# Eight PSUM banks in two sets that change roles: T5 attention with its scores in two groups and the projections behind the weighing

## The reference, cut to what matters

```python
q = (hidden_states @ wq).reshape(b, s, H, DK).transpose(0, 2, 1, 3)   # k and v likewise; H=16, DK=64, s=512
scores = jnp.einsum('bhqd,bhkd->bhqk', q, k) + bias                   # bias by relative position and head
attn = softmax(scores)
out = jnp.einsum('bhqk,bhkd->bhqd', attn, v)
return out.transpose(0, 2, 1, 3).reshape(b, s, H * DK) @ wo
```

## Time and profile before

| | |
|---|---|
| median of 3 runs | 1156.37 us (1152.84 to 1157.34) |
| the profiled execution | 1156.04 us, of which the span of its instructions 1154.2 us |
| mean granted TensorE clock | 0.997 |
| PE, DVE, ACT, POOL busy over the span | 97%, 79%, 80%, 54% |
| attention, from W0(0) to W0(29) | 60.48 to 402.15 us |

### The profile page before, as it was taken

The page is one execution under the profiler, slowest core; times in us unless marked ns, Lnnn a source line. Parts: engine busy times, 40 slices in busy tenths (PEclk is TensorE's granted clock), DMA queues, the critical chain, the costliest instruction groups (busy, mean ns, idle before and its releaser), DMA issues.

```text
span 1154.2 us, 40441 instructions
## 1 busy us (share of the span) xinstructions
PE 1121.6 (97%) x16041; PEld 721.5 (63%) x16041; DVE 911.5 (79%) x2424; ACT 924.6 (80%) x2455; POOL 617.7 (54%) x406
## 2 busy tenths in 40 slices
PE   8899999999999998999999999999999899999998
PEld 3367777677776763666666666555556566666665
DVE  4798989999999978887777777867778777777774
ACT  5887877777787868887888888887888788888975
POOL 4466666566666644764564555433353455655540
PEclk9999999999999999999999999999999999999999
DMA  8411111111111122311111111011010111110110
GB/s 276 172 39 40 58 41 54 44 49 49 40 58 40 57 74 63 93 38 31 31 44 42 29 43 34 20 34 33 19 42 20 35 28 43 43 42 20 43 43 20
DMA packets 30364, 58.36 MB, mean 51 GB/s; under 512 B 5680, under 2 KB 7152, under 8 KB 30176
## 3 DMA queue, kind: packets, MB, share of 16 engines
q1 hardware_dynamic: 30176, 55.77, 17.9%
HBM read 15.32 MB, written 1.11 MB: 14 GB/s over the span
## 4 chain that ended last, share of the span: by engine, by line
PE 83%; ACT 8%; issue 4%; DVE 3%; POOL 1%; DMA 1%; SPq 0%; DVEq 0%; ACTq 0%; POOLq 0%
PE ps L326 11%; PE ps L301 11%; PE ps L1501 6%; PE ps L1425 5%; PE ps L1458 5%; PE ps L1362 5%; PE ps L1372 4%; PE ps L1395 4%; PE ps L1363 4%; PE ps L1437 4%; PE ps L1465 4%; PE ps L337 3%; PE ps L1507 3%; ACT arena L1725 3%; PE ps L267 2%
## 5 line engine op out<-in xcount | busy, mean ns | idle before, releaser
L241 POOL TENSOR_TENSOR arena<-arena 128x1024 f32<-128x1024 f32 x128 | 241.0, 1893 | 144.9 <-DVE arena L536 144.8
L1302 POOL TENSOR_TENSOR arena<-arena 128x1024 f32<-128x1024 f32 x64 | 121.4, 1897 | 225.8 <-DVE arena L1903 225.8
L432 ACT ACTIVATE arena<-arena 128x512 f32<-128x512 f32 x256 | 182.4, 713 | 73.8 <-DVE arena L522 73.4
L1725 ACT ACTIVATE arena<-arena 128x128 f32<-128x128 f32 x512 | 198.2, 390 | 16.3 <-DVE arena L1895 15.7
L1895 DVE CUSTOM_DVE_ANT_0 arena<-ps,near,arena 128x128 f32<-128x128 f32 x512 | 144.5, 348 | 50.1 <-PE ps L1425 50.1
L522 DVE CUSTOM_DVE_ANT_0 arena<-ps,arena 128x512 f32<-128x512 f32 x256 | 164.3, 688 | 23.9 <-PE ps L301 21.1
L532 DVE STREAM_TRANSPOSE arena<-arena 128x1024 f32<-128x1024 f32 x128 | 157.8, 1234 | 1.1 <-POOL arena L241 0.9
L1309 POOL TENSOR_TENSOR arena<-arena 128x1024 f32<-128x1024 f32 x64 | 151.0, 2359 | 0.1
L326 PEld LDWEIGHTS ps<-arena 32*64 32x64 f32 x8192 | 118.8, 130 | 37.2 <-issue 36.7
L301 PE MATMUL ps<-arena 64*128 64x256 f32 (+1 forms) x736 | 138.4, 488 | 2.0 <-DVE arena L522 1.4
L326 PE MATMUL ps<-arena 32*64 32x128 f32 x8192 | 134.8, 274 | 0.5 <-issue 0.4
(11 more groups left out here) (164 smaller groups left out, 2179.0 us busy)
## 6 DMA issues: line engine op xcount, KB each, us to landing
arena<-arena SPq DMA_DIRECT2D x127, 128.0 KB, 2.3
arena<-arena SPq DMA_DIRECT2D x64, 192.0 KB, 2.6
arena<-rel_rows SPq DMA_DIRECT2D x16, 448.0 KB, 9.3
arena<-arena SPq DMA_DIRECT2D x64, 64.0 KB, 2.1
arena<-y SPq DMA_DIRECT2D x30, 128.0 KB, 2.3
arena<-arena SPq DMA_DIRECT2D x15, 127.8 KB, 2.4
arena<-in_wqkv SPq DMA_DIRECT2D x2, 768.0 KB, 5.1
x<-in_x SPq DMA_DIRECT2D x4, 256.0 KB, 4.7
```

Of the source, the lines that this page charges most:

```text
L241: nc.gpsimd.tensor_tensor(e, e, scale, ALU.mult).then_inc(self.normed, 1)
L432: nc.scalar.activation(self.e[:, r % 3, i, :], self.neg[:, i, :], ACT.Exp, bias=self.nmax[:, i:i + 1], scale=-1.0, accum_out=self.sums[:, ...
L1302: nc.gpsimd.tensor_tensor(e, e, self.rsum.unsqueeze(2).to_broadcast([P, H8, P]), ALU.mult).then_inc(self.p_normed, 1)
L1725: nc.scalar.activation(self.e[:, s, h, :], self.neg[:, h, :], ACT.Exp, bias=self.nmax[:, h:h + 1], scale=-1.0, accum_out=self.sums[:, s, h ...
```

## The change

The eight banks become two sets of four, `T5_S` and `T5_W`, whose roles depend on the unit. In slot u one set X takes the weighed output of unit u-1, the other set Y the scores of round r. When the biases of round r have read Y, its banks take Q, K, V(u+2) and PO(u-1). When out-copy(u-1) has read X, all four scores of round r+1 go to X. Unit 31 is excepted and stays in `T5_W`.

On PE both pairs of round r+1 stand together at the end of the slot, and Q, K, V come directly behind W1, ahead of PO. On ACT, exp(r+1,0) and exp(r+1,1) move behind the copies of q, k, v, and the two half copies of v move behind exp(r+1,3), as a function of their own. On DVE, from slot 1 on, four biases stand together in each round, the turns are shifted later by half a round, and add(u-1) stands ahead of bias(r+1,0) to bias(r+1,3). The closing slot's own order on DVE goes. The number of instructions for the arithmetic is the same.

```diff
+    def weigh_home(self, u):
+        return T5_S if u % 2 and u < self.LAST else T5_W
+    def score_home(self, r):
+        slot = r // 2 - 1
+        if slot <= 0:
+            return T5_S
+        return self.weigh_home(slot - 1) if r % 2 else self.other_home(slot)
+    def other_home(self, slot):
+        return T5_W if self.weigh_home(slot - 1) == T5_S else T5_S
...
         def q_proj(u):
-            if u >= 1:
+            if 1 <= u <= 2:
                 pe.wait_ge(self.q_read, u)
+            if u >= 3:
+                pe.wait_ge(self.biased, 8 * (u - 1) + 1)
+            Q = self.proj_banks(u)[0]
...
         def score(r, pair):
+            home, slot = self.score_home(r), u - 1
+            if pair == 0 and r % 2 and slot >= 1:
+                pe.wait_ge(self.ot_made, slot)
...
-                    if r >= 1 and c.start == 0:
+                    if r >= 1 and c.start == 0 and not (r % 2 and slot >= 1):
                         pe.wait_ge(self.biased, 4 * (r - 1) + i + 1)
...
         def weigh(u, half):
-                elif u >= 1:
-                    pe.wait_ge(self.added, u)
+                elif u == self.LAST - 1:
+                    pe.wait_ge(self.biased, 4 * (2 * self.LAST) + 3)
...
+                    if c == 0 and a == self.GROUPS - 1 and 1 <= u < self.LAST:
+                        pe.wait_ge(self.added, u)
...
-        def project_out(u, bank=T5_W):
+        def project_out(u):
             pe.wait_ge(self.ot_made, u + 1)
+            if u < self.LAST - 1:
+                pe.wait_ge(self.biased, 8 * (u + 2) + 4)
...
             if u >= 1:
                 weigh(u - 1, 1)
-            if scores:
+            if u == -1:
                 score(r + 1, 0)
-            if u >= 1:
-                project_out(u - 1)
             if u + 2 < self.UNITS:
                 q_proj(u + 2)
                 k_proj(u + 2)
                 v_proj(u + 2)
+            if u >= 1:
+                project_out(u - 1)
+            if u >= 0:
+                score(r + 1, 0)
             if scores:
                 score(r + 1, 1)
...
+        for u in range(1, self.UNITS - 1):
+            r = 2 * (u + 1)
+            if u >= 2:
+                invert_sums(r - 1, 0)
+                turn(r - 2, 1)
+                invert_sums(r - 1, 1)
+            for i in range(4):
+                add_bias(r, i)
+            invert_sums(r, 0)
+            if u >= 2:
+                turn(r - 1, 0)
+            turn(r - 1, 1)
+            invert_sums(r, 1)
+            turn(r, 0)
+            add_out(u - 1)
+            for i in range(4):
+                add_bias(r + 1, i)
+
+        r = 2 * (self.UNITS - 1)
+        invert_sums(r + 1, 0)
+        turn(r, 1)
+        invert_sums(r + 1, 1)
+        turn(r + 1, 0)
```

More of the change, by code:

```diff
@@ L218, in __init__, with proj_banks, out_bank @@
         self.weighed, self.ot_made, self.o_made, self.added = sem("weighed"), sem("ot_made"), sem("o_made"), sem("added")
+        self.LAST = self.UNITS - 1
         self.done, self.last = self.added, self.UNITS
+    def weigh_home(self, u):
[7 more added lines that the diff above has]
+        return T5_W if self.weigh_home(slot - 1) == T5_S else T5_S
+    def proj_banks(self, u):
+        slot = u - 2
+        first = T5_W + 1 if slot <= 0 else self.other_home(slot)
+        return tuple(self.k.ps[:, first + j, :] for j in range(3))
+    def out_bank(self, u):
+        if u >= self.LAST - 1:
+            return T5_W if u == self.LAST else T5_S + 3
+        return self.other_home(u + 1) + 3
     def sp(self, sp):
@@ L246, in pe @@
         k, nc, ps = self.k, self.k.nc, self.k.ps
-        Q, K, V = (ps[:, T5_W + j, :] for j in range(1, 4))
         ahead = self.ahead
@@ L325, in weigh @@
                         cols = slice(h * DK, (h + 1) * DK)
-                        last = nc.tensor.matmul(ps[cols, T5_W + a, 0:P], self.v[rows, u % 3, (a - c) % self.GROUPS, c // self.GROUPS, cols],
+                        last = nc.tensor.matmul(ps[cols, home + a, 0:P], self.v[rows, u % 3, (a - c) % self.GROUPS, c // self.GROUPS, cols],
                                                 self.pt[rows, u % 2 * 2 + h, :, keys],
@@ L412, in copy_k @@
                 act.wait_ge(self.scored, 8 * (u - 1))
-            nc.scalar.activation(self.kk[:, u % 2, :], K, ACT.Copy).then_inc(self.k_read, 1)
+            nc.scalar.activation(self.kk[:, u % 2, :], self.proj_banks(u)[1], ACT.Copy).then_inc(self.k_read, 1)
         def copy_v(u):
@@ L461, in act @@
                 exp(r, 3)
+            if scores and u < 0:
                 exp(r + 1, 0)
@@ L469, in act @@
                 copy_v(u + 2)
+            if scores and u >= 0:
+                exp(r + 1, 0)
+                exp(r + 1, 1)
             if scores:
@@ new lines, in add_out @@
+            nc.vector.tensor_tensor(xb, ps[:, self.out_bank(u), :], xb, ALU.add).then_inc(self.added, 1)
+        for u in range(-1, 1):
+            r = 2 * (u + 1)
+            for i in range(4):
+                add_bias(r, i)
+                if u == -1 and i == 0:
+                    ahead.norm4.scale(dve, 1)
+            if u == -1:
+                ahead.norm4.scale(dve, 2)
+            invert_sums(r, 0)
+            if u == -1:
+                ahead.norm4.scale(dve, 3)
+            else:
+                turn(r - 1, 1)
+            invert_sums(r, 1)
+            add_bias(r + 1, 0)
+            add_bias(r + 1, 1)
+            turn(r, 0)
+            invert_sums(r + 1, 0)
+            turn(r, 1)
+            add_bias(r + 1, 2)
+            add_bias(r + 1, 3)
+            turn(r + 1, 0)
+            invert_sums(r + 1, 1)
```

77 lines of the change are left out of this document (25 added, 52 removed).

## The result

The changed kernel takes 1149.86 us (median of 6 runs, 1148.11 to 1151.9), the kernel before beside it 1156.86 us (6 runs, 1152.84 to 1159.67). The ratio is 0.9935, with an interval of 0.9921 to 0.9950: faster by 0.65%, 7.0 us. The forecast was 1149.0.

The account below looks back on a forecast made before the run. PE was taken to set the pace, with DVE next. From 1156.04 us, -6.1 (steady slots), -2.0 (start) and +0.95 (end) sum to -7.15, giving 1148.9, written as 1149.0 us after a 0.33 us median offset; range 1146.5 to 1153.

Parts of the forecast that it names:

- What bounds the kernel: Steady slots: PE is gapless and sets the pace, a tiling switch costs about 0.2 us, DVE comes next.
- Part 1: Steady slots 1 to 29: five tiling switches instead of six save 0.21 us each, -6.1 us.
- W0 2.03: Steady slots: the first weighing block keeps its old length of 2.03 us in the new order.
- New waits in the steady slots: Steady slots: PE's new waits on DVE and ACT cost nothing; DVE waits at two places, about 0.9 us.
- the cover of 1.1 us: Steady slots: smallest margin before PE would wait for DVE, 1.1 us, at the add and at bias(r+1,3).
- Part 2: Start of attention: Q, K, V(2) fill PE's 1.44 us wait for a bias; -2.0 us, bounds -0.3 and -2.2.
- 1.5 for the order: Start: with only the bound from bias(3,3), W1(0) starts at 62.9 instead of 64.42, 1.5 us earlier.
- 0.5 for the half copies: Start: half copies of v behind exp(1,3) let DVE come forward, raising the gain from 1.5 to -2.0 us.
- The bound of 61.9: Start: S(4,1) must wait for bias(3,3), starting at 61.20 before with its result 0.69 later.
- The clock's fall at the start: Start: rival, chance 0.15; the clock falls again there, 1.7 us come back, giving 1150.7 us.
- Part 3: End, slot 30: W1(30) starts 13.5 behind W0(29), 12.57 before; loses +0.95 us, bounds 0 and +1.5.
- the two reasons given: End: PO(29) waits 0.85 us for the out-copy, and centre(0) waits for bias(63,3), out at 12.5.

Follow-up runs that it names:

- e1: Changed kernel with the scores of round r+1 split around PO, putting two tiling switches back; 1160.44 us, ratio 1.0024 to the kernel before.
- e7: Changed kernel with one extra DVE addition of 128 x 512, result unused, behind the add in slots 1 to 30; 1150.35 us, ratio 0.9929.
- e8: Changed kernel with three extra DVE additions of 128 x 512, results unused, behind the add in slots 1 to 30; 1181.09 us, ratio 1.0205.
- e10: Changed kernel with 32 matmuls of 8 columns, results unused, added at the head of the kernel; 1161.22 us, ratio 1.0034.
- e12: Changed kernel with 32 unused matmuls of 8 columns at its head and turn(62,0) moved behind the last four biases; 1160.70 us, ratio 1.0033.
- e4: Changed kernel with PE's wait for add(u-1) at the head of W0 instead of its seventh matmul; 1151.16 us, ratio 0.9941.
- e9: Changed kernel with the attention matmuls that some units cut into halves of 256 columns issued whole; 1150.81 us, ratio 0.9930.
- e2: Changed kernel with PO moved directly behind W1, ahead of Q, K, V, still with five switches; 1176.08 us, ratio 1.0157.
- e5: Changed kernel with the two half copies of v directly behind copy_v again, in every slot; 1152.03 us, ratio 0.9952.
- e6: Changed kernel with turn(62,0), the last slot's third turn on DVE, moved behind the last four biases; 1149.90 us, ratio 0.9931.
- e3: Changed kernel with slot 0 alone back in the old order on PE and ACT, S(3,0) ahead of Q, K, V(2); 1151.19 us, ratio 0.9944.

## Why the prediction was right, and where its sizes were off

**What bounds the kernel.** Right. PE is gapless in both kernels, a switch costs 0.2 us (e1), and DVE is next (e7, e8).

**Part 1, 0.21 us per slot.** The mechanism is right, the size is not: 11.78 - 11.64 = 0.14. The shortest slot of the trace is 11.56, the forecast to the digit. The mis-sized step is "W0 2.03" and "W1 2.03", read from a kernel in which neither block has a gap between W0(1) and W0(29). After the change W0 takes 2.07 on average and W1 2.05, the scores some 0.02 more. These are two things. The W1 part is three gaps of 0.22 to 0.26 us, at 143.85, 213.86 and 248.94:

```profile
143.85 2.32 PE L362 MATMUL ps<-arena 32*64 32x128 f32 x128
146.09 1.13 PE L292 MATMUL ps<-y,arena 128*128 128x512 f32 x2
```

This block takes 2.24 us by starts. In each of the three the first late matmul comes 2.3 to 2.4 us behind the start of a transfer of 16 KB on the queue that the page calls "instruction". The first transfer starts at 142.45, and the late matmul at 144.73. The gap at 411.95 fits this too. That the gaps keep to places in the program is shown (e10, e12); that PE is short of instructions there is argued from this and from the transfers, and no run shows it directly. The W0 part, 0.03 to 0.08 us in most slots and nearly all in the last three records, is not the place of the wait (e4), not a late add (e1), not the number of instructions (e9, a third of it at most), and not the place in the program (e10 to e12). It is absent where PE pauses (e2) and where a single pair of scores stands ahead of W0 (e1, before). Its cause stays open.

**New waits in the steady slots: none.** Right, with the cover of 1.1 us measured as 1.13 and DVE's waits at 0.43 and 0.36. e7 shows that half of that room can be used up for nothing.

**Part 2, -2.0 us.** The sum is right, -1.93, and the mechanism too: PE's wait is filled, and then bias(3,3) sets the pace. Counted from S(2,0), bias(3,3) starts after 12.05 us in the kernel before (61.20 - 49.15) and after 11.42 in the changed one (60.69 - 49.27), which is the 0.6 us that the prediction took from half of the half copies. But its two terms, 1.5 for the order and 0.5 for the half copies, were mis-sized, and it is luck that they add up. With the half copies where they were, the new order wins only 15.27 - 15.00 = 0.3 us, although before's stretch holds the fall of the clock, since bias(3,3) then starts 13.19 us behind S(2,0) (e5); moving them wins the other 1.8. The bound of 61.9, read from the old order, does not hold in the new one without that move. The prediction's 51.7 for the start of Q(2) is a slip as well: 53.30 less 1.44 is 51.86, and Q(2) started at 51.92; the term does not hang on it.

The clock's fall at the start, a rival with 0.15, did not come in this execution. The granted clocks of the runs do not say where a fall stands: of 37 runs of the kernel before, 2 have a mean of 1.000, of the 6 of the changed kernel 4 (one stretch of 3.4 us lowers it by 3.4 x 0.5 / 1150 = 0.0015).

**Part 3, +0.95 us.** W1(30) starts 13.60 behind W0(29), 0.1 from the forecast, for the two reasons given. The term is +1.49 when counted to W1(31), since two gaps at "issue", 0.38 and 0.55 us, stand behind the point at which the prediction stopped counting. Before has such gaps there too, so only their difference counts: W1(30) to W1(31) takes 9.83 us before, 10.29 in the changed kernel, and 8.74 in e5, which has none. So the part beyond the forecast, about 0.5 us, belongs to this execution and not to the change.

**The sum.** The profiled execution is 6.2 us shorter, of which 1.67 are a fall of the clock late in the kernel that before's profile has and after's lacks. Without it the terms give -4.55 instead of -7.15: Part 1 misses by 2.0 us and Part 3 by 0.5. (The prediction's own sum with the 0.33 us of the median added is 1149.2, and not 1149.0.) Yet over the runs the difference is 7.0 us. The clock does not explain this: the eight runs of before with a mean granted clock of 0.999 or 1.000 have a median of 1157.1 us, the four of the changed kernel with 1.000 one of 1149.6. That is 7.5 us at equal clock, about 3 us more than the terms give. Where other executions lose or win these does not show in the two profiles and stays open. That 1149.0 met 1149.86 is in part luck: the terms that the two profiles show carry about two thirds of it.

**No better version.** e6, e7, e9, e3 and e4 lie within a measurement of the changed kernel. e5, at 0.9952, is above it by little more than that, the rest is above it clearly.

## What to carry to other kernels

On a gapless PE the order of the blocks still has a price: count the changes of tiling per iteration, read the price of one from blocks that differ only in their neighbours (here 0.2 us), and group blocks of one tiling, but keep independent work between a result and its copy out of PSUM (e2: without it 0.93 us are lost to win 0.2). When a block's length is carried from the old trace into a new, denser order, take it as a lower bound. Before trusting a difference of 2 us between two profiles, look where the granted clock fell in each.

## What was not expected of the hardware

- In dense blocks of small matmuls (128 records in 2.03 us) single steps from one record to the next take 0.17 to 1.41 us, where 0.02 is usual, 2.3 to 3.2 us behind the start of a 16 KB transfer of instructions. Their place moved by 64 records when 64 records were added some 400 us earlier (e10, e12). No such gap stood in before's 56 weighing blocks between W0(1) and W0(29).
- A full-array matmul of 8 columns takes 0.21 us per record at full clock, all of it the load of its weights. The loads of e10's 64 records, with no gap but the first:

```profile
3.78 13.56 PEld L2220 LDWEIGHTS ps<-y 128*128 128x128 f32 x63 [0.20 <-issue]
```

- The clock fell behind waits of PE of 1.44 us, 1.68 us (e5), 1.78 us (before, 911.12) and 1.99 us (e8, 432.53), and did not fall behind 1.78 us in the changed kernel (906.60), nor behind 1.17 us in e3. The same wait can go either way.
